# Recurrent block and mixture of experts on one core: the routing stage rebuilt around the prefix counts, the one-hots and the queue of the small loads

## The reference

```python
s = attn(xn)                 # xk, xv, xr = xn mixed with its shift by one token;
                             # k, v, r = three 256x256 projections; wkv scan over time; output Wo
logits = xn @ w_router.T     # 2048 tokens x 16 experts
probs = softmax(logits);  top_w, top_e = top_k(probs, 4);  top_w /= sum(top_w)
out = sum over experts e of coeff_e * (silu(xn @ w_gate[e]) * (xn @ w_up[e])) @ w_down[e]
x = x + s * silu(out)
```

## Time and profile before

| what | value |
| --- | --- |
| median of 3 runs | 364.33 us (363.87 to 364.96) |
| profiled execution, span | 374.3 us |
| PE busy | 310.6 us (83%) |
| DVE busy | 282.9 us (76%) |
| POOL busy | 227.3 us (61%) |
| ACT busy | 146.0 us (39%) |

### The profile page before, as it was taken

One profiled execution on the slowest core, in us unless ns is written; L12 is line 12 of the kernel. 1 busy time (PEld: TensorE's weight loads), 2 busy tenths in 40 slices (PEclk: granted clock), 3 DMA queues, 4 the chain that ended last, 5 costly groups with the idle time before them and its releaser, 6 DMA issues.

```text
span 374.3 us, 4815 instructions
## 1 busy us (share of the span) xinstructions
PE 310.6 (83%) x1162; PEld 183.0 (49%) x1163; DVE 282.9 (76%) x534; ACT 146.0 (39%) x222; POOL 227.3 (61%) x231
## 2 busy tenths in 40 slices
PE   0798968569899899999994999999999979959500
PEld 0343423234456465656562656566566546648400
DVE  3928999998469769699693599697796942259994
ACT  2545552411552452723631724625427213208121
POOL 5404559955637767765774477778667665327364
PEclk9999999988999999999999999999999989969955
DMA  7999900251512213422224122234222659174333
GB/s 248 300 343 348 345 5 0 90 164 44 154 42 83 84 48 94 143 78 70 73 78 135 42 84 80 79 93 132 73 79 85 213 189 331 48 234 125 133 112 113
DMA packets 37894, 48.81 MB, mean 130 GB/s; under 512 B 3756, under 2 KB 33453, under 8 KB 37872
## 3 DMA queue, kind: packets, MB, share of 16 engines
q1 hardware_dynamic: 30864, 30.43, 25.3%
q0 software_dynamic: 7008, 18.10, 15.2%
HBM read 35.94 MB, written 13.63 MB: 132 GB/s over the span
## 4 chain that ended last, share of the span: by engine, by line
PE 43%; DVE 33%; issue 8%; DMA 4%; POOL 3%; ACT 3%; another core or an unknown queue 2%; SPq 1%; DVEq 1%; POOLq 0%; ACTq 0%
PE ps L588 36%; DVE wbig L1042 6%; DVE ohA L924 5%; PE ps L690 3%; PE ps L677 3%; DVE ohB L922 2%; POOL y_rows L411 2%; DMA xg<-xn_rows,tok_idx 2%; DMA woT<-woT_in 2%; DVE arena L954 1%; POOL xg L404 1%; PE ps L597 1%; DVE arena L815 1%; DVE arena L949 1%
## 5 line engine op out<-in xcount | busy, mean ns | idle before, releaser
L588 PE MATMUL ps<-wbig,arena 128*128 x576 | 206.3, 499 | 10.6 <-DVE arena L949 6.8
L588 PEld LDWEIGHTS ps<-wbig,arena 128*128 128x128 f32 x576 | 105.2, 195 | 74.5 <-issue 67.4
L411 POOL DMA_INDIRECT y_rows<-arena,s_idx x56 | 62.2, 1110 | 42.3 <-ACT arena L541 25.5
L404 POOL DMA_INDIRECT xg<-xn_rows,g_idx x64 | 70.3, 1099 | 22.8 <-issue 17.0
L954 DVE TENSOR_TENSOR arena<-arena,ps 128x512 f32<-128x512 f32 x36 | 24.5, 682 | 41.9 <-ACT arena L536 25.9
L536 ACT ACTIVATE arena<-ps 128x512 f32<-128x512 f32 x36 | 21.5, 597 | 87.0 <-PE ps L588 53.2
L588 PE MATMUL ps<-arena 128*128 128x512 f32 x96 | 47.1, 638 | 1.0 <-DVE arena L815 1.0
L949 DVE COPY arena<-ps 128x512 f32<-128x512 f32 x36 | 24.8, 690 | 26.3 <-PE ps L690 18.2
L541 ACT COPY arena<-ps 128x512 f32<-128x512 f32 x36 | 21.1, 585 | 45.8 <-PE ps L588 35.9
L690 PEld LDWEIGHTS ps<-ident,arena 128*128 128x128 f32 x144 | 18.4, 145 | 22.6 <-issue 19.3
L588 PEld LDWEIGHTS ps<-arena 128*128 128x128 f32 x96 | 18.6, 202 | 21.5 <-issue 19.4
(11 more groups left out here) (151 smaller groups left out, 385.6 us busy)
## 6 DMA issues: line engine op xcount, KB each, us to landing
wbig<-y_rows SPq DMA_DIRECT2D x3, 2048.0 KB, 9.6
wbig<-wg_in SPq DMA_DIRECT2D x2, 2048.0 KB, 13.3
wbig<-wu_in SPq DMA_DIRECT2D x2, 2048.0 KB, 18.4
rT<-x_in SPq DMA_DIRECT2D x4, 512.0 KB, 6.0
xn_rows<-rT SPq DMA_DIRECT2D x4, 512.0 KB, 4.1
kT<-x_in SPq DMA_DIRECT2D x8, 256.0 KB
wbig<-y_rows SPq DMA_DIRECT2D x8, 256.0 KB, 5.2
out<-wbig SPq DMA_DIRECT2D x8, 256.0 KB, 2.1
```

The lines of the kernel that those rows point to most:

```text
L404: pool.indirect_dma_start(out=xg[:, par, j, :], out_offset=None, in_=xn_rows, in_offset=bass.IndirectOffsetOnAxis(ap=idx[:, n + j:n + j + ...
L411: pool.indirect_dma_start(out=y_rows, in_=ysb[:, par, j, :], in_offset=None, out_offset=bass.IndirectOffsetOnAxis(ap=idx[:, n + j:n + j + ...
L588: ins = nc.tensor.matmul(dst, lhsT(c), rhs(c), start=(c == 0), stop=(c == C - 1))
```

## The change

The logits are made by token: the transposed tokens are the stationary operand and the router's 16 columns the moving one, so the result needs no copy and no second transpose. The selection works on the logits themselves in PSUM, and the softmax moves behind the index tables, into `row_weights`. The running count over tiles is made by DVE on `sel_by_e` and added up over partitions by PE, with two accumulating matmuls after product 2 of `project(0)`; the slot search over 4 x 16 values gives way to a second `max` over `pos`. One comparison makes the `ohA` of two tiles (8 one-hots of 80), and the token's number is multiplied in on the side of `ohB`, on DVE and POOL. `RING` becomes 8, the placements move forward to `project(1)` and `project(2)`, and `mixes(2)` and `mixes(3)` move back (the last behind `index_ready`). Five small loads are issued by ACT instead of SP. `LATE`, the number of blocks of down weights that wait for `weights_ready`, goes from 5 to 7 (640 KB to 896 KB).

```diff
@@ POOL, the one-hots
-                if t == 2:
+                if t == 7:
                     add_before(2, 2)
-                if t == 12:
+                if t == 14:
                     add_before(3, 1)
...
-                    ins = pool.tensor_scalar(ohB[:, t % RING, s], iota_row, prow[:, t, s:s + 1], None, ALU.is_equal)
+                    ins = pool.tensor_scalar(ohB[:, t % RING, s], iota_row, prow[:, t, s:s + 1], val[:, 1 - s % 2, t:t + 1],
+                                             ALU.is_equal, ALU.mult)
@@ ACT
+            for dst, src in ((vec[:, :], vec_in), (wrou[:, :, :], wrouT_in.rearrange("(c p) n -> p c n", p=P))):
+                act.dma_start(dst, src).then_inc(route_in, 16)
+            for w, src in enumerate((wkT_in, wvT_in, wrT_in)):
+                act.dma_start(wT[w], src.rearrange("(c p) n -> p c n", p=P)).then_inc(proj_in, 16)
@@ PE, logits
-                product(ps[0:E, B_G + b, :], lambda c: wrou[:, c, :],
-                        lambda c: xnT[:, c, b, 1:SEQ + 1]).then_inc(lgt_psum, 1)
...
+                for t in range(b * TB, (b + 1) * TB):
+                    at_t = 1 + (t - b * TB) * P
+                    ins = product(logits[:, t, :], lambda c: xnT[:, c, b, at_t:at_t + P], lambda c: wrou[:, c, :])
                 ins.then_inc(logits_ready, 1)
@@ PE, counts and placements
-                if n == 3:
+                if n == 2:
+                    flat_sel = sel.rearrange("p t e -> p (t e)")
                     pe.wait_ge(sel_ready, 1)
...
+                    nc.tensor.matmul(ps[:, B_Y, 0:T * E], before, flat_sel, start=True, stop=False)
+                    pe.wait_ge(incl_ready, 1)
+                    nc.tensor.matmul(ps[:, B_Y, 0:T * E], ones, incl.rearrange("p e t -> p t e"), start=False, stop=True)
+                    nc.tensor.matmul(totals, ones, incl[:, :, T - 1], start=True, stop=True).then_inc(count_ready, 1)
...
-            project(1)
+            project(1, lambda n: place_rows((0, 0, 0, 1, 2, 2)[n]))
             count_ended()
-            project(2, lambda n: place_rows((0, 2, 2, 2, 2, 2)[n]))
-            project(3, lambda n: place_rows((3, 3, 0, 0, 0, 0)[n]))
+            project(2, lambda n: place_rows((2, 2, 2, 2, 3, 0)[n]))
+            project(3)
@@ DVE, from the logits to the digits
             dve.wait_ge(logits_ready, BATCH)
-            link(V.tensor_reduce(rmax, logits, X, ALU.max))
...
             for t in range(T):
-                ins = V.max(m8[:, t, :], prob[:, t, :])
+                ins = V.max(m8[:, t, :], logits[:, t, :])
...
+            link(V.tensor_tensor(sel_by_e.rearrange("p e t -> p t e"), gt, eq, ALU.add))
             V.tensor_tensor(sel, gt, eq, ALU.add).then_inc(sel_ready, 1)
+            V.tensor_tensor_scan(flat(incl), flat(keep), flat(sel_by_e), 0.0, ALU.mult, ALU.add).then_inc(incl_ready, 1)
...
+            dve.wait_ge(count_ready, 1)
+            link(V.tensor_scalar(ntilei, totals, float(P - 1), None, ALU.add))
...
+            link(V.tensor_tensor(pos, prefix, base_row.unsqueeze(1).to_broadcast([P, T, E]), ALU.add))
+            link(V.tensor_tensor(pos, pos, sel, ALU.mult))
+            for t in range(T):
+                ins = V.max(k8[:, t, :], pos[:, t, :])
@@ DVE, the one-hots
-                    mixes(3)
-                if t >= RING:
-                    dve.wait_ge(oh_used, t - RING + 1)
+                    mixes(2)
+                if t % 2 == 0:
+                    r = t % RING
+                    if t >= RING:
+                        dve.wait_ge(oh_used, t + 2 - RING)
+                    V.tensor_tensor(ohA[:, r:r + 2].rearrange("p r s n -> p (r s) n"),
+                                    iota16[:, 0:NT].unsqueeze(1).to_broadcast([P, 2 * TOPK, NT]),
+                                    ptile[:, t * TOPK:(t + 2) * TOPK].unsqueeze(2).to_broadcast([P, 2 * TOPK, NT]),
+                                    ALU.is_equal)
                 for s in range(dve_slots(t)):
-                    V.tensor_scalar(ohB[:, t % RING, s], iota16, prow[:, t, s:s + 1], None, ALU.is_equal)
-                for s in range(TOPK):
-                    ins = V.tensor_scalar(ohA[:, t % RING, s], iota16[:, 0:NT], ptile[:, t, s:s + 1], val[:, s % 2, t:t + 1],
+                    ins = V.tensor_scalar(ohB[:, t % RING, s], iota16, prow[:, t, s:s + 1], val[:, 1 - s % 2, t:t + 1],
                                           ALU.is_equal, ALU.mult)
                 ins.then_inc(ohA_ready, 1)
...
             V.tensor_scalar(tok_idx[:, 0:NT], dst_idx[:, :], TOK - 1, None, ALU.bitwise_and).then_inc(index_ready, 1)
+            mixes(3)
```

157 lines of the change are left out of this document (62 added, 95 removed).

## The result

The changed kernel takes 376.19 us (median of 4 runs, 373.92 to 377.41) where the kernel before takes 364.64 in the same series (4 runs, 363.87 to 366.26): a ratio of 1.0296, 95% interval 1.0255 to 1.0337. It is slower by 11 us; 364.3 was predicted.

What follows compares the result with a forecast made beforehand. PE bounds the main loop, untouched; the front is its last placement plus PE's work behind it. Placement 5.0 us earlier, 4.7 longer behind, 0.2 waiting: 93.3 - 93.5 + 0.2 = 0.0, so 364.3 us, range 360 to 370.

Steps and rivals of the forecast that it cites:

- The logits: Front, router products: 0.12 us per short matmul instruction, low clock until about 19.5; logits at 27.4, 1.5 us earlier.
- rival C: Logits: PE stays in the low clock through the short matmuls, 8.1 us or 2.5 more; 367 to 372 us; chance 13%.
- The clock after PE's waits: Half-clock products after PE waits: 3.3 us instead of 1.7 after the first placement, 2.9 for the last of `project(2)`.
- The digits: DVE's index work from the logits on: digits ready at 38.9 us, where it was 53.7.
- The first placement: Behind `project(1)`'s fourth product: PE stands still 6.3 us for POOL's addition and one-hots; placement at 55.2 us.
- POOL's one-hot: POOL's one-hots with a second operation and scalar: 0.70 us each, against 0.625 before.
- rival D: Second scalar makes POOL's one-hot dear: at 1.1 us each, 6.4 us longer, 370 us; chance 10%.
- Behind the last placement: `mixes(3)`, then all six products of `project(3)`: 13.4 us against 8.65, 4.7 longer, ending at 93.3.
- The load of 896 KB: Down weights behind `row_weights` (94.0): SP's load takes 5.0 us, until 99.1; 0.5 us of PE waiting, 0.2 taken.
- The end: Behind the front: PE-bound main loop untouched by the change, differences carried over to the median unchanged.
- The x loads: Start of the front: ACT's five loads run beside the x loads and delay them by 0.8 us, between 0 and 3.3.
- rival E: ACT's loads delay the last x loads by their whole length, 3.3 instead of 0.8 us: 366.8 us; chance 5%.

Runs made afterwards that it cites:

- the good one: Changed kernel with POOL's one-hots ahead of waiting additions, three of four ohB on DVE, mixes and waits moved: ratio 0.992; with old logits and 16 extra matmuls 0.977.

## Why the prediction was wrong, by its own steps

The last column is the changed kernel with the logits in the old way, where the logits are ready almost at the predicted moment.

| step | predicted | measured | with old logits |
| --- | --- | --- | --- |
| second set of transposes | 14.0 | 12.87 | 12.88 |
| logits ready | 27.4 | 31.5 | 27.6 |
| digits | 38.9 | 46.0 | 41.4 |
| `project(1)` starts | 42.0 | 47.43 | 44.59 |
| its fourth product ends | 48.9 | 56.3 | 51.7 |
| first placement | 55.2 | 63.17 | 59.70 |
| last placement | 79.9 | 89.15 | 87.81 |
| projections done | 93.3 | 103.1 | 102.9 |
| second pair | 98.6 | 110.36 | 109.96 |

Two steps failed: the clock through the logits, and the sum from the logits to the second pair, which was put at 71.2 us and took 78.9, and 82.4 with the old logits.

- **The logits.** "Twice that in the low clock. The low clock holds here ... until about 19.5" failed. The price in the low clock was near (0.20 us for a short matmul, 0.24 taken; no row shows one at the full clock), but the pace did not rise at 19.5; it was low until about 34.5, through the logits and the first product of `project(0)` (twelve instructions in 7.0 us, where twelve take 5.4 at the full clock). From the second transposes to the logits 13.4 us were predicted and 18.6 measured. It rose late because of the logits by token, as they alone in before's kernel show. This is rival C, at 13%, and it named the place and the price: "8.1 us, or 2.5 if the clock rises midway". The Trainium skill ("TensorE: Matmul & The Clock Gate", Part 1) says that the gate is set by how busy PE has been recently; here PE was busy for 18.43 of the 18.5 us from 12.8 to 31.3 and the pace of equal instructions stayed at half, so this stretch does not agree with the sentence.
- **What that was worth.** In the time of this kernel little: put right, it gives back 3.9 us at the logits and 0.4 at the second pair. With the logits in time the steps behind them (the last column) make the second pair 11.4 us late all the same. These are one profile each, and the moment at which the clock rises or falls in them differs by chance, so the 0.4 could as well be 0 or 2; that most of the 3.9 is gone is shown.
- **The clock after PE's waits.** The prediction charged it after the first placement and ahead of the last product of `project(2)`, and nowhere else. After PE's wait of 2.42 us ahead of `project(1)` (2.6 predicted) the granted clock was 0.50 from 48.4 to 50.4, and the four products took 8.85 us instead of 6.9: a term of 2 us that was put at nothing. With the old logits it falls twice further on, at 74.03 and behind the last placement (15.0 us where 13.4 were predicted).
- **The digits** came 3 us later than the logits did: 1.5 by the slow product ahead of the counts, and 1.8 since L837 took 1.98 us while POOL's addition ran from 43.51 to 45.51. `mixes(1)` would have stood for that addition in any case, as predicted, so the digits were not what set `project(1)`. With the old logits the collisions are others: from the logits to the digits it takes 13.8 us where 11.5 were predicted (DVE's L835 1.93 beside a POOL addition, 0.42 predicted), and POOL's addition ahead of the first one-hot takes 2.96 instead of 2.1.
- **The first placement** had the right form: PE stood still for 6.9 us (6.3 predicted), released by POOL's one-hot, and the granted clock was 0.5 after it. It moved with what stood before it. The wait is not itself the loss: without it (placements later) nothing came back in the time.
- **POOL's one-hot**, 0.70 taken, is 0.786. The term was mis-sized by 0.09: the 13 that lie on the path from the first to the last placement make 1.1 us. This is rival D, at the small end.
- **Behind the last placement** the products took 13.9 us where 13.4 were predicted. That step held.
- **The load of 896 KB** took 5.32 us (5.0 predicted from the earlier trace rows), but PE waited 1.6 us for it (0.2 predicted): `row_weights` ended at 104.6, since L883, an operation of three elements, stood for 2.33 us against POOL's last addition.
- **The end** was taken as unchanged and is 2.2 us shorter, which hides part of the error: without it the time would be further off.
- **The x loads** beside ACT's five were a small term. In the kernel with all loads on SP and no wait for woT the second transposes start at 12.40; in the profiles of the changed kernel and its variants at 12.81 to 13.99. The effect of rival E is 0.4 to 1.6 us there, half of its 3.3 at most.

The largest single error of the sum is the first, and it is not what decided. The prediction saw that "what is late next is not DVE but the chain product, ACT, POOL", and had its order right; it priced collisions and half-clock products at a few places only. In the runs they stood at most steps (the last column is 2 to 3 us later than predicted, step by step, at four of them), and the range gave them no more room than the bounds of two prices. (One slip of reading besides: the sixteen instructions in 8.65 us of the earlier trace rows are four products, not two.)

## What to carry to other kernels

A copy and a second transpose saved by computing with 16 columns at a time were paid for by PE's pace: before trading one 512-column matmul for many short ones, look whether PE has reached its full pace by then, and price what stands behind them at half of it too. Whether that shows in the time depends on what bounds the stretch behind: 3.9 us at the logits were worth 0.4 in the changed order and 6.5 were worth 5.9 in the good one. When work is taken from the bound engine, read what is queued ahead of the next engine's first useful instruction: here an addition that waited 7 us stood before one-hots that could have run, and putting the queues in order, with DVE taking its share back and the other moves of that kernel (not tried apart), turned 3.0% slower into 0.8% faster. A wait of 3 us without a releaser at one point of a loop's end is worth a try with a few instructions more or less.

## What the runs showed of the hardware that was not expected

- Eight one-column matmuls more in PE's program take away a wait of 2.9 to 3.5 us ahead of the last pair's second transposes. All six profiles with the old logits and nothing added have it, all nine with the logits by token don't, and the three with added matmuls don't. The profile names no releaser; that it depends on the code ahead of it is shown at three amounts (0, 8 and 16 more), what the engine waits for is not.
- PE at half pace through 18 us of back-to-back 16-column matmuls and transposes (12.87 to 31.34), with the granted clock's column at 1.00 in that stretch. That the clock is what was low is read from the pace of equal instructions (1.79 against 1.02 us for eight transposes); the column doesn't show it.
- The pace rises at different moments in executions of the same instructions: with the old logits the first router product takes 2.09 to 3.60 us in nine profiles, with the logits by token the first twelve instructions of `project(0)` take 7.0 to 8.4 in seven. That alone moves a front by up to 1.5 us, so positions of two profiles compare no more finely.
- On one chip the main loop had waits of 2 to 5 us scattered in it, in all four variants profiled there, for many of which the trace names no instruction of this core as releaser ("remote" or "issue"); before took 373.5 us there, 8 more than elsewhere. Why is open. The first profile of before has one of 4.7 us. Timeline of ACT in the logits-by-token kernel on that chip:

```profile
153.47 0.60 ACT L525 ACTIVATE arena<-ps 128x512 f32<-128x512 f32 x1 [6.75 <-remote]
```

- Making POOL's one-hots dearer (the second scalar) did not slow the front of before: the last placement ended at 81.4 instead of 84.4, of which 0.9 us stands at the logits already. It is one profile, and the cause is not shown.
- Operations of DVE with a single SBUF input stand too while POOL adds: L837 (128 x 64, int32) took 1.98 us and L883 (three elements) 2.33.
